# Condition matrices by pairs of rows, token tiles on two load queues, and ten warming products

## What is computed

```python
W = weights[condition]                       # one of 16 sets (64 x 64) for each of the 32 samples
y = jnp.einsum('bct,bcd->bdt', x, W)         # "conditioning"
h = gelu(jnp.einsum('bsd,df->bsf', y, inter_w) + inter_b)
out = x + jnp.einsum('bsf,fd->bsd', h, output_w) + output_b
```

## Time and profile before

| | |
|---|---|
| median of three runs | 1259.98 us (1259.71 to 1260.14) |
| the profiled execution | 1260.09 us |
| its span | 1258.3 us |
| PE busy | 1253.7 us (100% of the span) |
| DVE, ACT, POOL busy | 832.5, 567.3, 186.2 us |
| memory traffic over the span | 197 GB/s |

### The profile page before, as it was taken

The page is one execution under the profiler, slowest core; times in us unless marked ns, Lnnn a source line. Parts: engine busy times, 40 slices in busy tenths (PEclk is TensorE's granted clock), DMA queues, the critical chain, the costliest instruction groups (busy, mean ns, idle before and its releaser), DMA issues.

```text
span 1258.3 us, 15369 instructions
## 1 busy us (share of the span) xinstructions
PE 1253.7 (100%) x5662; PEld 1043.7 (83%) x5662; DVE 832.5 (66%) x1091; ACT 567.3 (45%) x969; POOL 186.2 (15%) x93
## 2 busy tenths in 40 slices
PE   9999999999999999999999999999999999999998
PEld 9888888888888888888888888888888888888887
DVE  5977787676577767656557455555547767784764
ACT  4744554454444444444434444444444444444442
POOL 4262223321000000000034233312200000000000
PEclk9999999999999999999999999999999999999999
DMA  9576655764997322249845324554189932323431
GB/s 345 164 269 248 246 196 221 277 251 181 388 389 278 101 88 96 101 171 358 306 147 183 104 117 170 184 184 148 75 332 394 347 136 91 101 101 100 155 130 52
DMA packets 94234, 249.28 MB, mean 198 GB/s; under 512 B 7344, under 2 KB 15824, under 8 KB 92752
## 3 DMA queue, kind: packets, MB, share of 16 engines
q1 hardware_dynamic: 93408, 248.01, 54.3%
q10 hardware_dynamic: 720, 0.28, 0.1%
q0 software_dynamic: 32, 0.00, 0.0%
HBM read 162.28 MB, written 85.98 MB: 197 GB/s over the span
## 4 chain that ended last, share of the span: by engine, by line
PE 99%; DVE 0%; DVEq 0%; issue 0%
PE ps L553 48%; PE ps L569 48%; PE ps L498 1%; PE ps L513 1%; PE ps L579 1%; DVE acc L873 0%; DVE acc L972 0%; DVEq L66 0%; DVE ones L903 0%
## 5 line engine op out<-in xcount | busy, mean ns | idle before, releaser
L553 PE MATMUL ps<-y,lhs 128*128 128x512 f32 x2688 | 611.0, 389 | 0.0
L569 PE MATMUL ps<-rhs,lhs 128*128 128x512 f32 x2688 | 609.6, 389 | 0.0
L569 PEld LDWEIGHTS ps<-rhs,lhs 128*128 128x128 f32 x2688 | 504.5, 188 | 104.8
L553 PEld LDWEIGHTS ps<-y,lhs 128*128 128x128 f32 x2688 | 504.1, 188 | 104.4
L705 ACT ACTIVATE lhs<-h_raw 128x512 fp32r<-128x512 f32 x224 | 141.6, 632 | 345.8 <-PE ps L569 340.1
L854 DVE TENSOR_TENSOR lhs<-h_raw,lhs 128x512 fp32r<-128x512 f32 x224 | 155.1, 692 | 188.4 <-ACT lhs L705 188.4
L795 DVE TENSOR_TENSOR lhs<-w_raw,lhs 128x512 fp32r<-128x512 f32 x128 | 117.5, 920 | 125.4 <-ACT lhs L633 125.2
L633 ACT ACTIVATE lhs<-w_raw 128x512 fp32r<-128x512 f32 x128 | 80.9, 633 | 169.5 <-PE ps L553 163.4
L857 DVE TENSOR_TENSOR rhs<-W,rhs 128x512 fp32r<-128x512 f32 x224 | 153.4, 685 | 0.0
L795 DVE TENSOR_TENSOR lhs<-s_w,lhs 128x512 fp32r<-128x512 f32 x96 | 91.2, 952 | 88.1 <-ACT lhs L633 88.1
L466 POOL TENSOR_TENSOR s_w<-w_raw 128x1024 f32<-128x1024 f32 x16 | 48.1, 3006 | 621.1 <-PE ps L569 354.0
(11 more groups left out here) (35 smaller groups left out, 293.2 us busy)
## 6 DMA issues: line engine op xcount, KB each, us to landing
h_raw<-h_mem SPq DMA_DIRECT2D x112, 512.0 KB, 3.3
w_raw<-in_L_ffn_inter_w_dram SPq DMA_DIRECT2D x32, 1024.0 KB, 8.7
h_mem<-hs SPq DMA_DIRECT2D x64, 512.0 KB, 4.6
W<-in_L_ffn_output_w_dram SPq DMA_DIRECT2D x32, 1024.0 KB, 12.4
h_mem<-c SPq DMA_DIRECT2D x48, 512.0 KB, 5.7
y_mem<-y_out SPq DMA_DIRECT2D x28, 512.0 KB, 3.1
y<-y_mem SPq DMA_DIRECT2D x7, 2048.0 KB, 13.0
acc<-in_x_dram SPq DMA_DIRECT2D x16, 512.0 KB, 8.5
```

The costliest lines, as they stand in the source:

```text
L553: last = nc.tensor.matmul(ps[:, bank, :], w[:, k, :], y[i][:, part, k, :], start=(i in FRESH and k == 0 and u == 0), stop=(k == KH - 1 and ...
L569: last = nc.tensor.matmul(ps[:, bank2(h, j, tb), :], lhs[s % RING][:, a, blk(tb)], rhs[r][:, w, :], start=(j in FRESH and q == 0 and u == ...
```

## The change

The channels of a sample are put on the partitions in another order: the even channels of both samples on partitions 0 to 63, the odd ones on 64 to 127. The rows of a condition set follow: its even rows go to one 32-partition block of `wdiag`, its odd rows to another, so a pick is two copies of 32 x 64. `cond_all` holds two neighbouring rows of a set on a partition (32 partitions, runs of 512 bytes), at another address. Each tile of x is loaded by two transfers of 64 partitions: in pass 0 the even half by SP's queue and the odd one by ScalarE's, there ahead of b1; in pass 1 both by SP's. The 16 picks of pass 0 are shared by GpSimd and VectorE; ScalarE picks the first four of pass 1 and GpSimd the other twelve. The whole of `wdiag` is set to zero, pass 0's part by VectorE and pass 1's by GpSimd. Ten warming products stand in place of fifteen.

```diff
-    WARM = 15
+    WARM = 10
+    x_con = x.rearrange("(h j s) (q r) t -> h j r (s q) t", h=PASSES, s=PER, r=2)
-    cond_sets = cond_w.rearrange("s c d -> c s d")
+    cond_pairs = cond_w.rearrange("s (q r) d -> q s (r d)", r=2)
-        cond_all = at("cond_all", 204, [SETS, C])[0:C]
+        cond_all = at("cond_all", 80, [SETS, 2 * C])[0:C // 2]
 def pick(engine, i):
-            rows = slice(s * C, (s + 1) * C)
-            return wdiag[rows, j:j + 1, rows], cond_all[:, bass.ds(which, 1), :]
+            cols = slice(s * C, (s + 1) * C)
+            return [(wdiag[(PER * r + s) * C // 2:(PER * r + s + 1) * C // 2, j:j + 1, cols],
+                     cond_all[:, bass.ds(which, 1), r * C:(r + 1) * C]) for r in range(2)]
+        EVEN, ODD = slice(0, P // 2), slice(P // 2, P)
 SP
-            sp.dma_start(cond_all[:, 0:SETS // 2], cond_sets[:, 0:SETS // 2]).then_inc(cond_in, 16)
-            sp.dma_start(x0[:, 0, 0:BANK], x_tok[0, :, 0, 0:BANK]).then_inc(x0_half, 16)
-            sp.dma_start(x0[:, 0, BANK:D], x_tok[0, :, 0, BANK:D]).then_inc(x0_in[0], 16)
+            sp.dma_start(cond_all[:, 0:SETS // 2], cond_pairs[:, 0:SETS // 2]).then_inc(cond_in, 16)
+            sp.dma_start(x0[EVEN, 0, 0:BANK], x_con[0, 0, 0, :, 0:BANK]).then_inc(x0_half, 16)
+            sp.dma_start(x0[EVEN, 0, BANK:D], x_con[0, 0, 0, :, BANK:D]).then_inc(x0_in[0], 16)
             for j in range(1, TILES):
-                sp.dma_start(x0[:, j, :], x_tok[0, :, j, :]).then_inc(x0_in[j], 16)
+                sp.dma_start(x0[EVEN, j, :], x_con[0, j, 0]).then_inc(x0_in[j], 16)
             load_w1(0, 0)
             for j in range(TILES):
                 if j == TILES - 2:
                     sp.wait_ge(cond_done, 2 * KB)
-                sp.dma_start(x1[j][:], x_tok[1, :, j, :]).then_inc(x1_in[j], 16)
+                for r, rows in enumerate((EVEN, ODD)):
+                    sp.dma_start(x1[j][rows], x_con[1, j, r]).then_inc(x1_in[j], 16)
 GpSimd
-            nc.gpsimd.memset(wdiag[0:C, :, C:P], 0.0).then_inc(wdiag_zero, 1)
-            nc.gpsimd.memset(wdiag[C:P, :, 0:C], 0.0).then_inc(wdiag_zero, 1)
+            nc.gpsimd.memset(wdiag[:, TILES:PASSES * TILES, :], 0.0).then_inc(wdiag1_zero, 1)
...
+            for i in range(0, TILES * PER, 2):
+                for to, of in pick(pool, i):
+                    nc.gpsimd.tensor_copy(to, of).then_inc(picked[0], 1)
+            pool.wait_ge(picked[0], TILES * PER)
+            for i in range((TILES + 2) * PER, PASSES * TILES * PER):
+                for to, of in pick(pool, i):
+                    nc.gpsimd.tensor_copy(to, of).then_inc(picked1[0], 1)
 TensorE
-                    pe.wait_ge(x0_in[j] if j else x0_half, 16)
-                    for e in range(3):
-                        pe.wait_ge(picked[e], len(range(e, PER * (j + 1), 3)))
+                    pe.wait_ge(x0_in[j] if j else x0_half, 32)
+                    for e in range(PER):
+                        pe.wait_ge(picked[e], 2 * (j + 1))
...
-                pe.wait_ge(x1_in[j], 16)
-                pe.wait_ge(picked1, PER * (j + 1))
+                pe.wait_ge(x1_in[j], 32)
+                if j < 2:
+                    pe.wait_ge(picked1[1], 2 * PER * (j + 1))
+                else:
+                    pe.wait_ge(picked1[0], 2 * PER * (j - 1))
 ScalarE
-            act.dma_start(cond_all[:, SETS // 2:SETS], cond_sets[:, SETS // 2:SETS]).then_inc(cond_in, 16)
+            act.dma_start(cond_all[:, SETS // 2:SETS], cond_pairs[:, SETS // 2:SETS]).then_inc(cond_in, 16)
+            act.dma_start(x0[ODD, 0, 0:BANK], x_con[0, 0, 1, :, 0:BANK]).then_inc(x0_half, 16)
+            act.dma_start(x0[ODD, 0, BANK:D], x_con[0, 0, 1, :, BANK:D]).then_inc(x0_in[0], 16)
+            for j in range(1, TILES):
+                act.dma_start(x0[ODD, j, :], x_con[0, j, 1]).then_inc(x0_in[j], 16)
             act.dma_start(b1_rows[0:F // P], b1.rearrange("(a p) -> a p", p=P)).then_inc(b1_in, 16)
...
-            for i in range(1, TILES * PER, 3):
-                to, of = pick(act, i)
-                nc.scalar.activation(to, of, ACT.Copy).then_inc(picked[1], 1)
+            act.wait_ge(wdiag1_zero, 1)
+            for i in range(TILES * PER, (TILES + 2) * PER):
+                for to, of in pick(act, i):
+                    nc.scalar.activation(to, of, ACT.Copy).then_inc(picked1[1], 1)
 VectorE
             nc.vector.memset(ones[:], 1.0).then_inc(ones_made, 1)
+            nc.vector.memset(wdiag[:, 0:TILES, :], 0.0).then_inc(wdiag_zero, 1)
...
-            for i in range(2, TILES * PER, 3):
-                to, of = pick(dve, i)
-                nc.vector.tensor_copy(to, of).then_inc(picked[2], 1)
+            for i in range(1, TILES * PER, 2):
+                for to, of in pick(dve, i):
+                    nc.vector.tensor_copy(to, of).then_inc(picked[1], 1)
             dve.wait_ge(b1_in, 16)
```

More of the change, by code:

```diff
@@ L131, in build @@
         ones_made = sem("ones_made")
-        wdiag_zero = sem("wdiag_zero")
-        picked = [sem(f"picked_{e}") for e in ("pool", "act", "dve")]
-        picked1 = sem("picked1")
+        wdiag_zero, wdiag1_zero = sem("wdiag_zero"), sem("wdiag1_zero")
+        picked = [sem(f"picked_{e}") for e in ("pool", "dve")]
+        picked1 = [sem(f"picked1_{e}") for e in ("pool", "act")]
         s_made = [sem(f"s_made{i + 1}") for i in range(4)]
@@ L432, in _ @@
             pool.dma_start(itok_sb[0:1], itok.rearrange("(o b) -> o b", o=1)).then_inc(itok_in, 16)
-            nc.gpsimd.memset(wdiag[0:C, :, C:P], 0.0).then_inc(wdiag_zero, 1)
-            nc.gpsimd.memset(wdiag[C:P, :, 0:C], 0.0).then_inc(wdiag_zero, 1)
+            nc.gpsimd.memset(wdiag[:, TILES:PASSES * TILES, :], 0.0).then_inc(wdiag1_zero, 1)
             pool.wait_ge(itok_in, 16)
             pool.wait_ge(cond_in, 32)
[L437 to L448, removed]
+            pool.wait_ge(wdiag_zero, 1)
+            pool.wait_ge(wdiag1_zero, 1)
+            for i in range(0, TILES * PER, 2):
[5 more added lines that the diff above has]
+                    nc.gpsimd.tensor_copy(to, of).then_inc(picked1[0], 1)
+            pool.wait_ge(picked1[0], 2 * (TILES - 2) * PER)
             for h in range(PASSES):
@@ L489, in cond @@
                 for j in range(n * TB, (n + 1) * TB):
-                    pe.wait_ge(x0_in[j] if j else x0_half, 16)
-                    for e in range(3):
-                        pe.wait_ge(picked[e], len(range(e, PER * (j + 1), 3)))
+                    pe.wait_ge(x0_in[j] if j else x0_half, 32)
+                    for e in range(PER):
+                        pe.wait_ge(picked[e], 2 * (j + 1))
                     for kb in range(KB):
                         if j == 0 and kb == KH:
-                            pe.wait_ge(x0_in[0], 16)
+                            pe.wait_ge(x0_in[0], 32)
                         if j == TB:
@@ L579, in _ @@
                 nc.tensor.matmul(ps[:, i % 2, 0:P], ones[:, 0:P], ones[:, P:2 * P], start=True, stop=True)
-            pe.wait_ge(wdiag_zero, 2)
             for n in range(2):
@@ L750, in _ @@
                         if (h, g) == (0, 0) and c in (3, 5, 7, 8, 10):
+                            if c == 8:
+                                act.wait_ge(picked1[0], 2 * (TILES - 2) * PER)
                             y_high({3: 2, 5: 3, 7: 4, 8: 5, 10: 6}[c])
@@ L903, in _ @@
             nc.vector.memset(ones[:], 1.0).then_inc(ones_made, 1)
+            nc.vector.memset(wdiag[:, 0:TILES, :], 0.0).then_inc(wdiag_zero, 1)
             dve.wait_ge(itok_in, 16)
             dve.wait_ge(cond_in, 32)
-            for i in range(2, TILES * PER, 3):
-                to, of = pick(dve, i)
-                nc.vector.tensor_copy(to, of).then_inc(picked[2], 1)
+            dve.wait_ge(wdiag_zero, 1)
+            for i in range(1, TILES * PER, 2):
+                for to, of in pick(dve, i):
+                    nc.vector.tensor_copy(to, of).then_inc(picked[1], 1)
             dve.wait_ge(b1_in, 16)
```

## The result

| | before | after |
|---|---|---|
| median | 1259.85 us (1259.55 to 1260.14, 4 runs) | 1270.74 us (1268.82 to 1272.42, 4 runs) |
| ratio | | 1.0086, 95% interval 1.0069 to 1.0103 |
| profiled execution | 1260.09 us, span 1258.3 | 1271.88 us, span 1270.1 |
| rate of the loads, 8 to 22 us | 402 GB/s | 300 GB/s |

The forecast was 1262.8 us with a range up to 1265.3. The direction and one mechanism (b1 behind x0 in ScalarE's queue, VectorE waiting for it, TensorE waiting for VectorE) are in the profile as told. The size is not: the loss is four times the forecast.

A forecast was written before the change was run, and what follows sets the result against it. TensorE's gapless chain was taken to bound the kernel; b1's landing at 15.6 us moves the conditioning's end from 21.93 to 24.7, so 1260.09 + 2.8 = 1262.9, or 1262.8 us on the median; range 1259.0 to 1265.3.

The forecast's parts named there:

- b1 behind x0: ScalarE's queue: b1 lands at 15.6 us behind nine x0 loads, VectorE and TensorE wait, conditioning ends at 24.7, +2.8 us.
- What bounds the kernel: TensorE's chain alone, without a gap: whatever moves the conditioning's end at 21.93 us moves the kernel's end by as much.
- the step from the last odd half to b1: ScalarE's queue: b1 lands with the last x0 half, 0.1 to 0.3 us more for b1 itself and the 64-partition loads.
- this case's 58%: The stall as told, +2.4 to +3.8 us, 1262.4 to 1263.8; 36 put above the 1262.5 limit, 22 below.
- the 4.44 MB moved in the first 14.2 us: Transfer engines before the change: 14.2 us at 313 GB/s, taken as condition sets, x0 and b1 together.
- Part (4): Loads of x0: two queues deliver no sooner, condition sets save 0.3 us, 64-partition effect between 0 and 402 falling to 286 GB/s.
- halves that load slowly: Rival, 10%: x0 loads at 286 GB/s, b1 lands at 20.1, +7.3 us, 1267.3; half of that effect gives 1265.
- the 14 us that the prediction worked out for 196 GB/s: x0 loads: if both halves together ran at 196 GB/s, 4.46 MB need 22.8 us, end moves by an estimated 14.
- The clock: Rival, 13%: stall plus TensorE at 1.2 GHz behind it, 0.9 to 2.7 us more, together about 1264.6.
- the law: From b1's landing through VectorE's transposes and PSUM copies to the conditioning's end: 15.6 to 24.7, 9.1 us behind.
- the prediction's price for a spell: TensorE behind the stall: a slow-clock spell costs (1 - 0.1117/0.215) of its length, 0.9 to 2.7 us.
- Picks, zeroing, GpSimd's later sums, the early start: Before and during conditioning: first three cost nothing; TensorE starts at 6.3, 1.3 us sooner, spent in a wait.

The follow-up runs named there:

- TensorE kept at work: The changed kernel with 32 products of ones between the fourth and fifth conditioning tiles, b1 and all else kept; 1268.16 us.
- The trace of the loads alone: One execution of a separate kernel that computes nothing, loading eight tiles six times, each time in another shape; whole tiles 407 GB/s, partitions 0 to 63 217.
- its second profile: The changed kernel executed again without any edit; median 1269.34 us, the profiled execution 1267.57 us.

## Why the prediction was wrong, point by point

**What bounds the kernel: right.** Apart from the last stores, all that moved the end lay before the first product or, with b1 ahead of x0, in that product itself (3.1 us of slow clock). Behind it TensorE had no hole, in the kernel after or in any experiment that computes.

**b1 behind x0: right, and the path behind its landing too.** The forecast put the conditioning's end 9.1 us behind b1's landing. It was 9.34 both times the clock held (b1 behind x0 in the kernel before, and with TensorE kept at work). What was not right is the step from the last odd half to b1: taken at 0.1 to 0.3 us, together with all that the halves cost, it was 2.0 us in the kernel after, in which SP's even halves came last. The split of this case's 58% doesn't follow either: 22 of them were put below 1262.5, while its own bounds were 1262.4 and 1263.8. And the 4.44 MB moved in the first 14.2 us were not just the condition sets, x0 and b1, since the last tile landed at 15.6; by then 5.0 MB were through, some 0.5 of them w1's.

**The rate of the loads: the step that failed.** The term of the sum that was mis-sized is b1's landing, by the rate behind it. Part (4) bounded the effect of 64-partition transfers by 0 and by a fall from 402 to 286 GB/s, and took nearly nothing. Measured were 301 GB/s from 8 to 16 us and 300 from 8 to 22. b1 landed at 20.6 in place of 15.6, which is 5.0 us of the 7.1 between 2.8 and 9.93. The rate makes most of the 5.0: the 5.0 MB that had been moved by 15.6 us before the change were through at 20.0 us after it. The unlikely rival, halves that load slowly, had b1 at 20.1 and 1267.3 us, and was given 10%. Its b1 is near the measured one partly by luck, since it counted neither w1's bytes nor the 2.0 us behind the last odd half. The reason for the choice was that the only such rows in the trace were short ones, so that their 286 GB/s could be put down to the short rows. That was no evidence against the effect.

The Trainium skill has it ("SBUF — State Buffer", Door 1: The DMA port swizzle): partitions 0 to 63 reach half of the ports. The trace of the loads alone agrees: 217 GB/s for 0 to 63, where the Trainium skill gives 196 at 1 MiB and about 218 as the limit. And partitions 32 to 95, which by the Trainium skill's formula lie on both halves of the ports, landed in step with their issue. On two transfers at once, one to each half, the same page of the Trainium skill is plain ("Can I just issue two DMAs to hit both halves?"): only 6% more than one. Here they reached 7% more than 0 to 63 alone when issued in turn by one queue (233 GB/s against 217) and 23% more by two queues (267). From 8 to 16 us the kernels with halves ran at 271 to 309 GB/s, so the 14 us that the prediction worked out for 196 GB/s were too many.

**The clock: a rival that came together with another.** It was priced at 0.9 to 2.7 us with 13%, as a case of its own beside slow halves. But the longer b1 took, the longer TensorE stood: 6.8 us, where some 3 had been forecast. The traces have the fall over waits of 6.8, 6.7 (twice), 3.7, 3.0 and 2.8 us, and not over 3.36 and 2.55, so near 3 us either was seen. In the kernel after it cost 1.9 us (9.54 against 7.64 for the 62 matmuls), in its second profile 1.0. With the 0.24 by which the law was short, 2.8 + 5.0 + 1.9 + 0.24 = 9.94. The slow clock of the warming products, on which the prediction's price for a spell rests, is read from their spacing alone; the granted-clock column is 1.00 there (0 to 14.2 us).

**The last stores: not foreseen.** 1.87 us of the profiled execution, in which a fetch of instructions fell among the last stores. That the fetch is the cause is only argued: three profiles have stores of 3.9 to 4.0 us with a fetch among them, the same kernel's second profile has 2.1 us, and no run took the fetch alone away.

**Picks, zeroing, GpSimd's later sums, the early start: as told.** TensorE began at 5.88 in place of 7.48 (forecast 6.3) and spent the head start in waits; VectorE's picks were over at 11.7, sooner than the forecast's 13.9; GpSimd's first sum at 27.7 kept nobody waiting on the chain. The run with fifteen warming products fits that: no change of the time is seen.

**Which part costs what.** By the runs, b1's place in the queue costs 3.6 us with whole tiles (profiled execution; 5.5 by the medians) and 4.0 in the changed kernel; the halves by partitions cost 4.7 us in a kernel that is otherwise the same (by the chains; 6.4 by the medians); TensorE's clock behind a wait adds 1.9 us, and either of them can set it off. These costs are of different kernels and don't add up exactly: the changed kernel's own medians, 1270.74 and 1269.34, lie 1.4 us apart.

## What to carry to other kernels

In every run that had b1 behind x0, its 16 KB landed behind all of x0, 9.6 to 13.7 us after their issue. When loads move to another queue, look at what stood in it, and at what the engine itself still has to do behind its issues. Split a load by columns before you split it at partition 64: 389 GB/s against 271. And price rivals that lengthen the same wait together, with the clock's fall behind them, rather than as cases that exclude each other.

## What the runs showed of the hardware that was not expected

- Partitions 0 to 63 loaded at 217 GB/s, all 128 at 407, and the two halves on two queues at 267, with the transfer engines' share above 1.0 each time. A full share is no sign of a full rate.
- SP's issue of a transfer of 64 rows of 4 KB took 0.60 us, that of 128 such rows 0.44, and that of 128 rows of 2 KB 0.43: half the rows took longer to issue.
- b1's 16 KB landed 2.0 us behind the last transfer ahead of it in its own queue in one profile of the changed kernel, and 0.2 us behind in the other.
- Three of thirteen profiles of the full kernel end with stores of 3.9 to 4.0 us in place of 2.1, and in these a fetch of 20 KB of instructions falls among them.
